# Cross-network kernel: row numbers from the ids on their own partitions, filter loaded in one go, last fold on GpSimd, products four banks apart

## The reference: what is computed

```python
e = stack([tbl_f[ids[:, f]] for f in range(39)], axis=1)      # 512 x 39 x 16
xk = x0 = e
for W in (f0, f1, f2):
    z = einsum('bfd,bgd->bfgd', x0, xk).reshape(b, f * g, d)
    xk = einsum('bpd,pm->bmd', z, W)                          # 128 wide
    outs.append(xk)
z = sum(concatenate(outs, axis=1), axis=-1)                   # 512 x 384
h = relu(concatenate([z, dense_ctx], 1) @ W_top1 + b_top1)
h = relu(h @ W_top2 + b_top2)
y = h @ W_top3
```

## Time and profile before

| | |
|---|---|
| time, median of 3 runs | 704.47 us (702.53 to 704.82) |
| the profiled execution | 706.52 us, of which the span from first to last instruction is 704.7 us |
| PE busy | 654.0 us, 93% of the span |
| DVE busy | 600.2 us, 85% |
| POOL busy | 508.1 us, 72% |
| ACT busy | 382.1 us, 54% |
| DMA | 41.28 MB, mean 59 GB/s |

### The profile page before, as it was taken

How to read it: one execution, slowest core, us unless ns; L and a number is a source line. 1 busy time by engine, 2 the same in 40 slices (tenths; PEclk the granted TensorE clock), 3 DMA queues, 4 the chain that set the end, 5 groups by cost and what they waited for, 6 DMA issues and landing times.

```text
span 704.7 us, 11586 instructions
## 1 busy us (share of the span) xinstructions
PE 654.0 (93%) x2992; PEld 512.8 (73%) x2992; DVE 600.2 (85%) x2013; ACT 382.1 (54%) x1162; POOL 508.1 (72%) x466
## 2 busy tenths in 40 slices
PE   0279979999999999999999999999999999999997
PEld 0256757776767788787867778788777878788877
DVE  4279898999999999989679999999779898988670
ACT  1146554665656474746446565646457474655431
POOL 6747977797889888786769889786758878463320
PEclk9979989999999999999999999999999999999999
DMA  7527530303031211304030220404030130300000
GB/s 145 139 70 227 145 80 6 109 9 108 9 102 16 76 41 38 79 9 107 5 108 9 54 63 8 108 6 111 5 105 11 38 79 4 106 1 1 1 1 2
DMA packets 70517, 41.28 MB, mean 59 GB/s; under 512 B 47553, under 2 KB 55297, under 8 KB 70322
## 3 DMA queue, kind: packets, MB, share of 16 engines
q1 hardware_dynamic: 58530, 35.67, 18.8%
q10 hardware_dynamic: 6672, 3.58, 2.2%
q0 software_dynamic: 5248, 1.29, 1.8%
HBM read 38.55 MB, written 1.94 MB: 57 GB/s over the span
## 4 chain that ended last, share of the span: by engine, by line
PE 73%; DVE 12%; issue 5%; POOL 4%; ACT 3%; DMA 1%; another core or an unknown queue 1%; SPq 0%; DVEq 0%; POOLq 0%; ACTq 0%
PE y L842 18%; PE y L844 16%; PE y L843 16%; DVE scaled L733 9%; PE late L860 4%; PE side L849 4%; PE acc L813 3%; PE acc L819 3%; PE acc L814 3%; POOL emb_quads L452 2%; ACT scaled L562 2%; PE y L860 1%; PE late L871 1%; PE late L903 1%; DVE z L703 1%
## 5 line engine op out<-in xcount | busy, mean ns | idle before, releaser
L733 DVE SCALAR_TENSOR_TENSOR scaled<-y,x_rows,scaled 128x128 f32<-128x128 f32 x1728 | 471.5, 341 | 57.0 <-ACT scaled L562 32.5
L562 ACT ACTIVATE scaled<-y,x_rows 128x128 f32<-128x128 f32 x768 | 218.7, 367 | 228.9 <-PE y L844 210.9
L842 PE MATMUL y<-w_hi,x_parts 128*128 128x512 f32 (+1 forms) x640 | 284.1, 444 | 11.3 <-DVE scaled L733 7.2
L844 PE MATMUL y<-w_hi,x_parts 128*128 128x512 f32 (+1 forms) x640 | 250.4, 391 | 0.0
L843 PE MATMUL y<-w_lo,x_parts 128*128 128x512 f32 (+1 forms) x640 | 250.3, 391 | 0.0
L463 POOL TENSOR_TENSOR z_parts<-z,z_parts 117x512 fp32r<-117x512 f32 (+1 forms) x107 | 138.7, 1296 | 44.7 <-ACT z_parts L512 39.3
L842 PEld LDWEIGHTS y<-w_hi,x_parts 128*128 128x128 f32 x640 | 121.3, 190 | 62.9 <-DVE scaled L733 30.9
L452 POOL DMA_INDIRECT emb_quads<-in_small_tables_dram,quad_rows x144 | 139.2, 966 | 25.1 <-issue 11.8
L844 PEld LDWEIGHTS y<-w_hi,x_parts 128*128 128x128 f32 x640 | 121.1, 189 | 26.4
L843 PEld LDWEIGHTS y<-w_lo,x_parts 128*128 128x128 f32 x640 | 121.9, 190 | 18.4
L471 POOL TENSOR_TENSOR sum<-scaled 128x512 f32<-128x512 f32 x64 | 83.2, 1300 | 69.5 <-DVE x_sb L741 59.8
(11 more groups left out here) (85 smaller groups left out, 370.9 us busy)
## 6 DMA issues: line engine op xcount, KB each, us to landing
z<-x_turned SPq DMA_DIRECT2D x320, 78.0 KB
x_three<-x_turned SPq DMA_DIRECT2D x48, 78.0 KB
x_turned<-emb_quads SPq DMA_DIRECT2D x156, 8.0 KB
w_sb<-in_w_dram SPq DMA_DIRECT2D x1, 2496.0 KB, 9.4
emb_quads<-in_small_tables_dram,quad_rows POOLq DMA_INDIRECT x144
s_sb<-in_w_dram ACTq DMA_DIRECT2D x28, 80.0 KB
x_turned<-emb_singles SPq DMA_DIRECT2D x95, 2.0 KB
wt_sb<-in_W_top_dram SPq DMA_DIRECT2D x1, 768.0 KB
```

Of the source, the lines that this page charges most:

```text
L562: done = act.activation(scaled[:, k % 2, BY_ACT.index(j), i * M:(i + 1) * M], y2[n % RING][:, i * M:(i + 1) * M], ACT.Copy, scale=x0_rows[ ...
L733: dve.scalar_tensor_tensor(part, y2[n % RING][:, i * M:(i + 1) * M], x0_f, part, ALU.mult, ALU.add).then_inc(terms_in, 1)
L842: pe.matmul(dst, x1_hi[:, t % 2, cols], hi, start=True, stop=False)
L844: pe.matmul(dst, x1_lo[:, t % 2, cols], hi, start=False, stop=True).then_inc(y_ready, 1)
```

## The change

Five things change. The row numbers of the quads are computed straight from `ids_sb`, where tile q of a group lies on partitions 32q to 32q+31; `table_at` therefore holds every place on all partitions. That takes 14 instructions for each q: 56 for the first group, one semaphore step per q, and 56 for the other three groups, which now stand ahead of `w0_lo` at the start; the loads of all ids are the first two transfers of SP's queue, and the eight into `ids_four` are gone. The filter is loaded by 16 transfers, ahead of all stores, in four pieces of every fourth field; its four high parts stand ahead of `three(0)` on ACT, its four low parts ahead of the products on DVE, and PE waits for all of them once. POOL folds 256 to 128 columns right after its own fold. The products stand at slots 0, 4, ... 24, and `x1_high` at slot 34 (was 31). The first three single gathers of group 1 move from tile 3's share to tile 2's.

```diff
-CHUNKS_AT = (0, 4, 7, 11, 14, 18, 21)
+CHUNKS_AT = (0, 4, 8, 12, 16, 20, 24)
-X1_AT = 31
+X1_AT = 34
...
-    cuts = (0, 0, 0, 0, len(SINGLES)) if g == 1 else (0, 0, 0, 3, len(SINGLES))
+    cuts = (0, 0, 0, 3, len(SINGLES))
...
+        def load_filter(queue, j):
+            for a in range(4):
+                r, n = (a - j) % 4, (F - j + 3) // 4
+                queue.dma_start(w1_raw[32 * a:32 * a + 32, j:F:4, :],
+                                w1[32 * j:32 * j + 32, r:SPLIT * (n - 1) + r + 1:SPLIT, :]).then_inc(w1_in[j], 16)
...
# POOL, in fold_three
                 pool.tensor_tensor(sum2[:, :], sum4[:, 0:2 * M], sum4[:, 2 * M:4 * M], ALU.add).then_inc(two_in, 1)
+                pool.wait_ge(two_in, k + 1)
+                if k >= 2:
+                    pool.wait_ge(s_ready, k - 1)
+                pool.tensor_tensor(x2_sb[:, k % 2, :], sum2[:, 0:M], sum2[:, M:2 * M], ALU.add).then_inc(x2_in, 1)
...
# ACT, at the start
-            load_filter(act, 0)
+            for j in range(W1_PIECES):
+                load_filter(act, j)
...
-            load_filter(act, 1)
-            act.wait_ge(w1_in[0], 256)
-            for i in range(W1_EARLY):
-                high_filter(i)
+            for j in range(W1_PIECES):
+                act.wait_ge(w1_in[j], 64)
+                copy(w1_hi[:, j:F:4, :], w1_raw[:, j:F:4, :]).then_inc(w1_hi_in, 1)
...
# DVE
+            def quad_numbers(groups, q):
                 for j in range(FPB):
                     for a, b, f in alike(j):
                         done = dve.tensor_tensor(
+                            quad_rows[SPT * j:SPT * j + SPT, groups, q, a:b],
+                            ids_sb[SPT * q:SPT * q + SPT, groups, f:f + 4 * (b - a - 1) + 1:4],
+                            table_at[SPT * q:SPT * q + SPT, j:j + 1, a:b].to_broadcast(
+                                [SPT, groups.stop - groups.start, b - a]), ALU.add)
...
-                    if s % BANKS == X2_AT and n > BANKS:
-                        x2_of(n // BANKS - 1)
-                    if t == 1 and s == REST_AT:
-                        dve.wait_ge(rest_ids_in, 80)
-                        quad_numbers(slice(TPG, TILES)).then_inc(quads_rest, 1)
```

More of the change, by code:

```diff
@@ L95 @@
 Y_AT = 149
[L99 to L102, removed]
+W1_PIECES = 4
 def runs(fields):
@@ L289, in cross_network @@
         weights_in = sem("weights_in")
-        w1_in = [sem(f"w1_in_{h}") for h in range(2)]
+        w1_in = [sem(f"w1_in_{j}") for j in range(W1_PIECES)]
         top_in = sem("top_in")
@@ L393, in _ @@
             sp.dma_start(ids_sb[:, 0, :], ids[0:P, :]).then_inc(ids_in, 16)
-            for j in range(4):
-                sp.dma_start(ids_four[32 * j:32 * j + 32, 0:TPG, :],
-                             ids[0:P, :].rearrange("(t p) f -> p t f", p=SPT)).then_inc(four_ids_in, 16)
+            sp.dma_start(ids_sb[:, 1:GROUPS, :], ids[P:B, :].rearrange("(g p) f -> p g f", p=P)).then_inc(rest_ids_in, 16)
             for u in range(TILES):
@@ L409, in _ @@
                 if u == 1:
[L410 to L413, removed]
                     sp.dma_start(w2_sb[:, :, :], w2).then_inc(w2_in, 16)
@@ L447, in quad @@
                 n = len(QUADS[i])
-                if u == TPG and i == 0:
-                    pool.wait_ge(quads_rest, 1)
+                if i == 0 and u < TPG:
+                    pool.wait_ge(quads_first, u + 1)
+                if i == 0 and u == TPG:
+                    pool.wait_ge(quads_rest, TPG)
                 if u >= 2 and i == 0:
@@ L512, in copy @@
                 return act.activation(dst, src, ACT.Copy)
-            def high_filter(i):
-                cut = slice(W1_CUTS[i], W1_CUTS[i + 1])
-                copy(w1_hi[:, cut, :], w1_raw[:, cut, :]).then_inc(w1_hi_in, 1)
             def rows(u):
@@ L686, in tables_begin_at @@
                     for j, f in enumerate(fields):
-                        done = dve.memset(table_at[SPT * j:SPT * j + SPT, 0, i:i + 1], small.index(f) * CHUNKS * ROWS)
+                        done = dve.memset(table_at[:, j, i:i + 1], small.index(f) * CHUNKS * ROWS)
                 return done
@@ L760, in _ @@
             dve.wait_ge(tables_begin, 1)
-            dve.wait_ge(four_ids_in, 64)
-            quad_numbers(slice(0, TPG)).then_inc(quads_first, 1)
+            dve.wait_ge(ids_in, 16)
+            for q in range(TPG):
+                quad_numbers(slice(0, 1), q).then_inc(quads_first, 1)
             dve.wait_ge(weights_in, 48)
@@ L767, in _ @@
             dve.memset(diag[:, :, :, :, :], 0.0).then_inc(no_diag, 1)
+            dve.wait_ge(rest_ids_in, 16)
+            for q in range(TPG):
+                quad_numbers(slice(1, GROUPS), q).then_inc(quads_rest, 1)
             dve.wait_ge(w0_hi_in, 1)
             dve.tensor_tensor(w0_lo[:, :, :], w0_raw, w0_hi[:, :, :].bitcast(F32), ALU.subtract).then_inc(w0_lo_in, 1)
-            for i in range(W1_EARLY):
+            for i in range(W1_PIECES):
                 second_filter_low(i)
@@ L832, in layer2 @@
                 f = fields_of(j)
-                if n < BANKS:
-                    pe.wait_ge(w1_hi_in, sum(1 for at in W1_CUTS[:-1] if at <= f[-1]))
-                    pe.wait_ge(w1_lo_in, sum(1 for at in W1_CUTS[:W1_EARLY + 1] if at <= f[-1]))
-                    if f[-1] >= W1_CUTS[W1_EARLY + 1]:
-                        pe.wait_ge(w1_lo_pool, 1)
                 cols = slice(k % NBLK * P, k % NBLK * P + P)
@@ L928, in _ @@
             pe.wait_ge(rows_in, 1)
+            pe.wait_ge(w1_hi_in, W1_PIECES)
+            pe.wait_ge(w1_lo_in, W1_PIECES)
             for t in range(TILES):
```

48 lines of the change are left out of this document (8 added, 40 removed).

## The result

The changed kernel takes 711.19 us (median of 6 runs, 708.12 to 712.51) where the kernel before takes 704.3 beside it (6 runs, 701.21 to 704.82): a ratio of 1.0111, 95% interval 1.0093 to 1.013 (the ratios here are those on record, with their intervals; they are near the quotient of the two medians, here 1.0098, and not equal to it). It is slower by 1.1%. The forecast was 685.5 us. The profiled execution took 711.75 us, with a span of 709.6. One execution in all that follows was of the slow kind, the profiled one of e12 at 1288.33 us: its trace is not used, and without it e12's median is 700.33.

The account below looks back on a forecast made before the run. DVE was taken to set the pace in tiles 1 to 3, PE from tile 5 on. Terms -6.0 - 1.2 - 1.0 - 2.0 - 1.9 - 7.0 = -19.1 led from 704.47 to 685.5 us, range 677.5 to 697.

Parts of the forecast that it names:

- Row numbers out of tile 1, -6.0: Tile 1 loses DVE's 4.17 us, PE's wait and the slow clock, becoming like tile 3; start work is covered: -6.0 us.
- Filter, -1.2 and -1.0: Start: loading the filter in one go brings `three_ps` 1.2 us earlier; shorter DVE low parts and PE's wait give -1.0.
- the remote wait, -2.0: Start: the 5.71 us wait of unknown releaser shortens as traffic before it is partly cleared; bounds 0 and 7, taken -2.0.
- Tile 0, -1.9 (part 4): Tile 0: DVE loses a filter low part and three folds, 4.7 us; PE's floor of 38.3 limits the gain to -1.9.
- Fold on POOL, -7.0 (part 5): Tile loop: moving the fold to POOL frees DVE of work and port waits, and POOL fits, barely: -7.0 us together.
- tiles 1 to 3 come to PE's pace, -1.1 each: Tiles 1 to 3, within the fold's term: DVE no longer sets the pace, 3 x -1.1 us.
- Products four banks apart, 0 (part 6): Tile loop: spreads DVE's bunched products, adds no instruction; x1 three slots later costs only slack, 0.7 us left: 0.
- x1 late at each tile's start: Rival: 14 tile starts each wait 1.3 us for x1, giving 704, or 723 if the clock falls too; chance 0.06.

Follow-up runs that it names:

- e12: Changed kernel with ACT's copy of s first, PE's transposes at slot 28 and the last fold back on DVE: 700.76 us, ratio 0.9940.
- e11: Changed kernel with products and x1 back, later row numbers before the weights wait, and the last fold back on DVE: 695.55 us, ratio 0.9906.
- e8: Kernel before with only the last addition of the fold moved from DVE to GpSimd: 700.62 us, ratio 0.9965.
- e9: e7 with the second group's five single gathers all in tile 1 again, as in the kernel before: 693.71 us, ratio 0.9861.
- e10: Changed kernel with products and x1 back on their old slots, same file as e2 on another chip: 693.26 us, ratio 0.9855.
- e1: Kernel before with only the products four banks apart and x1 at slot 34: 725.88 us, ratio 1.0258.
- e5: Changed kernel again, nothing edited, on another chip: 710.23 us, ratio 1.0104.
- e3: Changed kernel with ACT's copy of s put ahead of the high part in each slot: 717.83 us, ratio 1.0148.
- e13: Same file as e3, run again in another group: 717.20 us, ratio 1.0137.
- e6: e3 with PE's transposes of the rows at slot 28 instead of 27: 700.96 us, ratio 0.9971.
- e15: e6 with DVE's sum over x1 moved to slot 3 of the next tile: 707.90 us, ratio 1.0011.
- e7: Changed kernel with products and x1 back, later groups' row numbers computed before DVE's wait for the weights: 693.59 us, ratio 0.9866.
- e2: Changed kernel with products and x1 back on their old slots, everything else as changed: 707.38 us, ratio 0.9995.
- e18: Same file as e7, on a chip with gaps at the start: 709.02 us, ratio 1.0025.
- e16: e7 with DVE's sum over x1 moved to slot 3 of the next tile: 709.90 us, ratio 1.0039.
- e4: Changed kernel with the seventh product at slot 23 instead of 24: 717.27 us, ratio 1.0141.
- e17: Changed kernel with products and x1 back, later groups' row numbers computed in tile 1 at slot 6: 711.55 us, ratio 1.0051.

## Why the prediction was wrong

1. **Row numbers out of tile 1, -6.0:** the number right, its cause only in part. Tile 1 is 37.10 us in e11 (x2 on DVE as before) against 43.36, -6.3. But e11 also has three single gathers out of this tile. With all five in it, as in the kernel before, taking the row numbers out gives 3.1 us (43.15 in e8, 40.02 in e9): PE then waits for GpSimd's low part instead. The other 2.5 us are the gathers' move, and tile 0 pays 2.4 for it (e9 against e10). That the number came out is in part luck: the tile became one like tile 3 only because gathers left it too. No run has this comparison with x2 on DVE. The duration at the start, 109 ns each (measured 103 to 106), was right in the traces without gaps. In the others it was wrong by far: the second batch takes over 20 us instead of 6.
2. **Filter, -1.2 and -1.0, and 3. the remote wait, -2.0:** together 4.2, and the start shrank by 5.9 in the two profiled executions. But 4.2 of these are not the change's: the start of the kernel before is 44.6 in e8 (which differs from it in the fold alone) and 48.7 to 48.8 in the earlier trace rows and e1. What the change itself gives there is 1.6 to 1.8 us (44.56 in e8 to 42.93 in e5 on the same chip, 42.80 in the changed kernel's own trace). `three_ps` came 0.5 us earlier, not 1.2. Pricing the remote wait as something that the change's traffic could shorten was the error: e8 has the old loads and not this wait. The filter alone was not run.
3. **Tile 0, -1.9 (part 4):** wrong sign. It is 1.6 to 3.1 us longer (41.82 in e5, 43.31 in the changed kernel's own trace, against 40.22). PE's waits in slot 16 for GpSimd's low part are 0.3 us before, 0.85 with x2 there alone, 1.7 to 2.0 with three single gathers brought forward as well. The prediction looked at DVE's load in this tile and not at GpSimd's queue, and it passed over the change in `gathers_of`. Without that one (e9) the tile takes 39.42 us, 0.8 less than before.
4. **Fold on POOL, -7.0 (part 5):** the mechanism right, the size at most half: -2.3 to -3.6 us (e8, e11). The instruction takes 0.459 us where 0.456 was worked out. By the rule of the Trainium skill ("GPSIMD Engine Reference", section 4.1: about twice slower than VectorE) the estimate was 0.56; measured is 1.6 times DVE's 0.28, and the row decides for the line through the earlier trace rows. What failed is "tiles 1 to 3 come to PE's pace, -1.1 each": tile 3 is 36.93 in e10, -0.46, and tiles 4 and 8 gain nothing (38.24), since GpSimd's low part is late there in slot 19. DVE lost 2.0 us of work a tile, but PE waits for single banks in bursts (0.4 us in slot 11, 0.7 in slots 37 and 38), not for DVE's sum over the tile.
5. **Products four banks apart, 0 (part 6):** this is the step that failed. "No instruction is added ... its price is slack" looked at one consumer, x1 at the tile's end. It cost 15.1 us in tiles 1 to 14 (e5 against e10; 17.4 on the kernel before, e1), of which 12.7 go with three edits. ACT's high part of the seventh chunk fell ahead of the copy of s in slot 26 (e3, e13: 5.6 us). The contraction that covered ACT's slot 26 moved to slot 28 (e6: 4.1 us more). And DVE's sum over x1 stands right before the next tile's first banks (e15: 3.0 us more). The 2.4 us left are in tiles 4 and 8, which take 5.0 us more than in e10 while the others take 2.6 less: e15 waits there for GpSimd's low part in slot 28 (1.6 and 1.4 us), and 2.2 us come with the fallen clock. All three are waits of the order that the table sets, and the first two can be read from the order without a duration: what stands in ACT's slot 26, and what PE has between slot 26 and slot 27.

The sum of what the runs measured without gaps, tile 1, start, fold, tile 0 and products, is roughly -6.3 - 1.8 - 3 + 2 + 15 = +6; the changed kernel is 6.9 us slower. The terms overlap by up to 1 us (part of tile 0's loss is the fold's), and the last stretch differs by 3 us with the clock from one execution to the next, so nothing finer can be added up. The rival "x1 late at each tile's start" had the sign and nearly the time (704 to 723) and the wrong place: at the tile's start PE waits 0.9 us in tiles 2 to 4, 8 and 12 and 0 to 0.6 in the others after tile 1, and it waits for DVE's banks, not for x1; the rest is in slot 27. Left out of the forecast altogether was any look at `HIGH_LAG` and `CONTRACT_LAG` against `S_LAG` and `ROWS_AT`.

The best version is the changed kernel with the products where they were (e10, and with the row numbers at once e7 and e9): 0.9855 to 0.9866 on the two chips without gaps. On the three with them it is 0.9995 (e2), 1.0025 (e18) and, with the sum moved, 1.0039 (e16), so it isn't a version to take everywhere. Row numbers in fewer instructions at the start were not tried.

## What to carry to other kernels

A table that sets when work is issued sets an order on every engine. When an entry moves by three slots, list for each engine what now stands ahead of which waited-for instruction, and what work no longer lies between a producer and its consumer; slack at the end of the tile says nothing about either. Freed work on an engine that is busy 96% of the time pays only as far as the others wait for it at single points; count those waits, not the busy share. When such a wait goes, look for the next one behind it: here GpSimd's stood behind DVE's row numbers. And run a variant beside the unchanged kernel on more than one chip before its time decides about a theory: here two right repairs looked like failures.

## What the runs showed of the hardware

In three of the five groups, each on a chip of its own (e1 to e4, e13 to e16, e17 and e18), the start is held up by something that the profile doesn't name. In the changed kernel's variants it shows as stops among DVE's short int32 instructions, 18 to 22 us in all. In e17 and e1, and in the trace of the kernel before, which compute no later row numbers then, `x_rows` waits 5.6 to 5.9 us for a remote releaser instead. Whatever came before, the last stop or that wait ends at 35.2 to 36.4 us of the span in every one of these traces, and the tiles behind it are as long as in the other traces. In the traces of the other two groups, and in the changed kernel's own, there is neither. What holds the engines until then stays open: moving the row numbers earlier (e16, e18) or out (e17) changed which instruction is stopped and not when it ends. Whether it belongs to the chip or to the time stays open too.

In slot 16 of tile 0 PE waits for GpSimd's low part in the changed kernel and most variants. In four traces it waited 2.0 us, and behind it the granted clock fell to 0.50: the tile takes 43.31 to 43.35 us at a mean of 0.92 (the changed kernel, e7, e13, e15). In nine it waited 1.7 us and the clock stayed at 1.00: 41.82 to 41.89 us (e5 and e10 among them). The same file is found on both sides (the changed kernel and e5, e13 and e3, e7 and e18), so which of the two comes is not a matter of the code. The length of the wait does not decide alone: in tile 4 the clock fell behind 1.6 us of waiting in e15 and did not behind 1.8 in e6.
